# Causal input stage: q, k and v as three rounded products, parts from PSUM, gate logits first, v copied by ScalarE

## The reference, cut to what matters

```python
x = x + s * g                      # s: chunk attention, g: gate of layer 2
xn = _layernorm(x, axis=-1)
# attention of layer 3, input side
qkv = jnp.einsum('btd,ed->bte', xn, w_qkv)
q, k, v = ...                      # 16 heads of 16 channels
# expert choice of layer 3, input side
scores = jnp.einsum('ntd,ed->nte', xn, gate_w)      # 8 experts
probs = jax.nn.softmax(scores, axis=-1)
```

## Time and profile before

| | |
|---|---|
| median of three runs | 3751.04 us |
| profiled execution | 3749.36 us, span 3747.6 us |
| mean granted TensorE clock | 0.908 |
| TensorE, DVE, ScalarE, GpSimd busy | 85%, 81%, 61%, 49% of the span |
| the stage | first instruction at 1662.1 us, the next stage's at 1886.2 |
| first q_parts store of the first and the last batch | 1729.80, 1865.92 |
| DMA packets of the kernel | 478.20 MB, mean 128 GB/s |

### The profile page before, as it was taken

One profiled execution on the slowest core, in us unless ns is written; L12 is line 12 of the kernel. 1 busy time (PEld: TensorE's weight loads), 2 busy tenths in 40 slices (PEclk: granted clock), 3 DMA queues, 4 the chain that ended last, 5 costly groups with the idle time before them and its releaser, 6 DMA issues. The chain is left out here.

```text
span 3747.6 us, 55393 instructions
## 1 busy us (share of the span) xinstructions
PE 3170.5 (85%) x16305; PEld 1686.1 (45%) x16305; DVE 3029.9 (81%) x4822; ACT 2298.3 (61%) x2738; POOL 1834.0 (49%) x915
## 2 busy tenths in 40 slices
PE   6848998888997997878879999899997877777776
PEld 4522333333336886655523434389995631211111
DVE  6969999999995776865669897577768868888887
ACT  5867666667773334743446666522225659999998
POOL 0249998989993111011200000034434448999996
PEclk9879999999998998987879999999998978788888
DMA  3652233333312345955742333134435733344442
GB/s 124 243 203 107 102 146 148 147 124 120 146 49 77 113 150 159 215 140 187 253 139 73 79 73 87 45 95 89 89 62 181 227 115 104 119 124 121 123 119 85
DMA packets 313745, 478.20 MB, mean 128 GB/s; under 512 B 50839, under 2 KB 256280, under 8 KB 293134
## 3 DMA queue, kind: packets, MB, share of 16 engines
q1 hardware_dynamic: 256894, 408.82, 34.2%
q10 hardware_dynamic: 44432, 51.10, 5.1%
q0 software_dynamic: 12288, 16.79, 2.7%
HBM read 322.48 MB, written 153.91 MB: 127 GB/s over the span
## 5 line engine op out<-in xcount | busy, mean ns | idle before, releaser
L1235 PE MATMUL mamba_psum<-mamba_hc,scan_ident 128*128 128x512 f32 x1024 | 552.1, 648 | 86.4 <-DVE mamba_hc L1143 68.6
L3656 POOL TENSOR_TENSOR distance_dist<-distance_dist,distance_least_all 128x2048 f32<-128x2048 f32 x124 | 559.0, 4540 | 77.1 <-DMA distance_least_all<-distance_least_rows 77.1
L1166 DVE TENSOR_TENSOR_SCAN mamba_psum<-mamba_psum,mamba_drive 128x512 f32<-128x512 f32 x352 | 415.4, 1218 | 24.5 <-issue 10.3
L2793 DVE TENSOR_REDUCE causal_row_max<-causal_psum 128x1 f32<-128x512 f32 x512 | 333.3, 683 | 84.7 <-PE causal_psum L2863 71.0
L1235 PEld LDWEIGHTS mamba_psum<-mamba_hc,scan_ident 128*128 128x128 f32 x1024 | 178.1, 197 | 415.4 <-DVE mamba_hc L1143 248.9
L2752 ACT ACTIVATE causal_probs<-causal_psum 128x1024 f32<-128x1024 f32 x256 | 250.7, 1021 | 125.5 <-PE causal_psum L2886 123.6
L3832 PE MATMUL distance_psum<-distance_shared_k_stacks,distance_shared_q_stacks 102*128 102x512 bf16 x512 | 210.8, 508 | 115.0 <-DVE distance_least L3750 55.3
L3750 DVE TENSOR_REDUCE distance_least<-distance_psum 128x2 f32<-128x1024 f32 x256 | 294.4, 1217 | 8.6 <-PE distance_psum L3832 8.4
L3786 DVE TENSOR_SCALAR distance_dist<-distance_psum 128x1024 f32<-128x1024 f32 x192 | 227.1, 1221 | 82.5 <-PE distance_psum L3847 82.5
L1130 ACT ACTIVATE mamba_psum<-mamba_dt,scan_a_neg 128x512 f32<-128x512 f32 x256 | 167.3, 683 | 139.8 <-DVE mamba_hc L1143 139.3
L1130 ACT ACTIVATE mamba_psum<-late_channels,scan_a_neg 128x512 f32<-128x512 f32 x256 | 167.2, 683 | 139.9 <-DVE mamba_hc L1143 129.3
(11 more groups left out here) (473 smaller groups left out, 8734.6 us busy)
## 6 DMA issues: line engine op xcount, KB each, us to landing
distance_least_all<-distance_least_rows SPq DMA_DIRECT2D x32, 1024.0 KB, 4.7
scan_b_all<-bc SPq DMA_DIRECT2D x16, 1024.0 KB, 4.7
scan_c_all<-bc SPq DMA_DIRECT2D x16, 1024.0 KB, 6.6
mamba_b_all<-bc SPq DMA_DIRECT2D x16, 1024.0 KB, 5.0
mamba_c_all<-bc SPq DMA_DIRECT2D x16, 1024.0 KB, 7.0
choice_w<-L_ffn_w SPq DMA_DIRECT2D x16, 1024.0 KB, 5.6
z<-mamba_in_z SPq DMA_DIRECT2D x8, 1024.0 KB, 4.0
xc<-mamba_in_xc SPq DMA_DIRECT2D x8, 1024.0 KB, 4.9
```

The source lines that it names most:

```text
L1166: dve.tensor_tensor_scan(out, bank, drive[:, n % DRIVES], 0.0, ALU.mult, ALU.add).then_inc(h_ready, 1)
L1235: pe.matmul(ps[:, Y_BANK + m % 2], ident[:, :], hc[:, n % PRODUCTS], start=False, stop=(s == DS - 1)).then_inc(y_summed, 1)
L2793: dve.reduce_max(row_max[:, g % 2, u:u + 1], ps[:, u % 2], AX.X).then_inc(a_max, 1)
L3656: pool.tensor_tensor(dist[:, g % 2, kt], dist[:, g % 2, kt], least_all[:, g % 2], ALU.subtract).then_inc(shifted, 1)
```

## The change

- q, k and v: each fp32 product becomes three products of rounded parts, w and xn as `TwoParts`. ScalarE makes a second, rounded copy of each transposed half of xn, DVE the low part.
- `Split` becomes `DirectSplit`: ScalarE casts a tile from PSUM to its high part, DVE subtracts it from PSUM; the fp32 copy in SBUF goes.
- The context is stored in two parts (rounded and rest, 16 rows a batch instead of 8), and one rounded product spreads it.
- The gate logits come first on TensorE in a body, and the rest of the softmax with them; the transposes of probs stand between the two halves of v.
- v is copied by ScalarE. The middle parts stand at the end of ScalarE's body. SyncE stores probs ahead of v.

The core of the diff:

```diff
+        w_parts = TwoParts(c, "w_qkv", [P, DT, 3 * D])
+        xn_parts = TwoParts(c, "xn_t", [P, DT, T])
-        split = Split(c, q_out, k_out)
+        split = DirectSplit(c, q_out, k_out)
...
@@ SyncE
-                    sp.wait_ge(v_copied, b * 2 + 4)
-                    sp.dma_start(token_tiles(v_out, b), ...).then_inc(v_stored, DMA)
                     sp.wait_ge(probs_copied, b + 2)
                     sp.dma_start(probs_out..., probs_t[:, :]).then_inc(probs_stored, DMA)
+                    sp.wait_ge(v_copied, b * 2 + 4)
+                    sp.dma_start(token_tiles(v_out, b), ...).then_inc(v_stored, DMA)
-                means.store_context(sp)
-                load_context(0)
+                sp.wait_ge(y_parts, 2)
+                for j, y_part in enumerate((means.x, means.y)):
+                    sp.dma_start(context_in[:, j * NC:(j + 1) * NC, :], y_part[:, :]).then_inc(means.stored, DMA)
+                sp.wait_ge(means.stored, 2 * DMA)
+                sp.dma_start(context[:, :], context_in[0]).then_inc(loaded, DMA)
...
@@ ScalarE
+                act.wait_ge(turned.copied, len(turned.pairs))
+                for m in range(DT):
+                    act.copy(w_parts.high[:, m], w_turned[m]).then_inc(w_parts.rounded, 1)
                 def turn_copies(b):
                     for m in range(DT):
                         act.wait_ge(xt_done, b * DT + m + 3)
                         act.copy(xn_t[:, m], ps[:, m]).then_inc(xt_copied, 1)
+                        act.copy(xn_parts.high[:, m], ps[:, m]).then_inc(xn_parts.rounded, 1)
                 def body(b, more):
+                    act.wait_ge(shifted, b + 2)
+                    act.activation(lg[:, :, :], lg[:, :, :], ACT.Exp).then_inc(gate_exp, 1)
+                    for n in range(2):
+                        act.wait_ge(qk_done, b * split.TILES + n + 1)
+                        split.act_high(act, b, n, ps[:, 2 + n])
                     if more:
                         ln.act(act, b + 1)
-                    for n in range(split.TILES):
+                    for n in range(2, split.TILES):
                         act.wait_ge(qk_done, b * split.TILES + n + 1)
-                        split.act(act, b, n, ps[:, 2 + n])
-                    split.act_middle(act, b)
-                    act.wait_ge(shifted, b + 2)
-                    act.activation(lg[:, :, :], lg[:, :, :], ACT.Exp).then_inc(gate_exp, 1)
+                        split.act_high(act, b, n, ps[:, 2 + n])
+                    act.wait_ge(turn_done, b + 1)
+                    act.wait_ge(probs_stored, b * DMA + DMA)
+                    act.copy(probs_t[:, :], ps[0:NE2, 1]).then_inc(probs_copied, 1)
+                    act.wait_ge(v_stored, b * DMA + DMA)
+                    for j in range(2):
+                        act.wait_ge(v_done, b * 2 + j + 1)
+                        act.copy(v[:, 2 * j:2 * j + 2, :, 0:HD], ps[:, 6 + j]...).then_inc(v_copied, 1)
                     if more:
                         turn_copies(b + 1)
+                    split.act_middle(act, b)
...
@@ DVE
                 def body(b, more):
+                    if more:
+                        round_context(b + 1)
+                    dve.wait_ge(gate_done, b + 1)
+                    dve.reduce_max(top[:, :], scores, AX.X).then_inc(gate_step, 1)
+                    dve.tensor_tensor(lg[:, :, :], scores, wide(top), ALU.subtract).then_inc(shifted, 1)
                     if more:
                         sums(b + 1)
+                    dve.wait_ge(gate_exp, b + 1)
+                    ...
+                    for n in range(2):
+                        split.dve(dve, b, n, ps[:, 2 + n])
+                    if more:
+                        normed(b + 1)
+                    for n in range(2, split.TILES):
+                        split.dve(dve, b, n, ps[:, 2 + n])
+                    if more:
+                        take_low(b + 1)
...
@@ TensorE
+                    pe.wait_ge(xn_parts.rounded, b * DT + DT)
+                    for i in range(TT):
+                        for m in range(DT):
+                            last = pe.matmul(ps[:, 0, i * NE2:(i + 1) * NE2], xn_t[:, m, i * P:(i + 1) * P], wg[:, m], ...)
+                    last.then_inc(gate_done, 1)
+                    pe.wait_ge(xn_parts.ready, b * DT + DT)
                     for n in range(split.TILES):
-                        split.bank_free(pe, b, n)
                         for m in range(DT):
-                            last = pe.matmul(ps[:, 2 + n], w_qkv[:, m, n * P:(n + 1) * P], xn_t[:, m], ...)
+                            last = three_passes(pe, ps[:, 2 + n], w_parts.both(...), xn_parts.both(...), m == 0, m == DT - 1)
                         last.then_inc(qk_done, 1)
```

More of the change, by code:

```diff
@@ L1943, with __init__ @@
     SELECTS = 4
-    def __init__(self, c, weights, means_in, out):
+    def __init__(self, c, weights, means_in):
         R = self.ROWS
-        self.weights, self.means_in, self.out = weights, means_in, out
+        self.weights, self.means_in = weights, means_in
         self.ident = c.sb("ident", [P, P])
@@ L2374, in stage_causal_in @@
         chunks = c.sb("chunks", [P, TT, D])
-        context = c.sb("context", [NC, D])
+        context = c.sb("context", [2 * NC, D])
+        context_r = c.sb("context_rounded", [2 * NC, D], F32R)
+        y_high = c.sb("y_high", [means.ROWS, D], F32R)
         gate = c.sb("gate", [P, TT, D])
@@ L2438, in body @@
                     if first_groups:
-                        sp.wait_ge(split.stored, (b + 1) * split.STORES * DMA)
+                        split.wait_stored(sp, b)
                         sp.wait_ge(v_stored, (b + 1) * DMA)
@@ L2458, in _ @@
                     sp.wait_ge(stored, (NB + 1) * DMA)
-                sp.wait_ge(split.stored, (NB + 1) * split.STORES * DMA)
+                split.wait_stored(sp, NB)
                 attention.rows_copied(sp)
@@ L2520, in fill @@
                     dve.wait_ge(filled, steps[0])
-                fill(chunk_of[:, :, :], 1.0)
+                for tile in ones:
+                    fill(tile, 1.0)
                 fill(v[:, :, :, :], 0.0)
@@ L2588, in _ @@
                 means.pe_attend(pe, ps)
-                pe.wait_ge(made, 2)
+                pe.wait_ge(made, MADE)
                 pe.sem_inc(xt_done, 2)
                 def spread_context(b):
-                    pe.wait_ge(loaded, (b + 1) * LOADS * DMA)
+                    pe.wait_ge(context_ready, b + 1)
                     for j in range(2):
                         for i in (2 * j, 2 * j + 1):
-                            last = pe.matmul(ps[:, 6 + j, i % 2 * D:(i % 2 + 1) * D], chunk_of[:, i], context[:, :], start=True,
+                            last = pe.matmul(ps[:, 6 + j, i % 2 * D:(i % 2 + 1) * D], chunk_of[:, i], context_r[:, :], start=True,
                                              stop=True)
@@ L3919, in build @@
     given2 = scratch("given2", (NB, T, D))
-    means, context = (scratch(n, (NB, NC, D)) for n in ("means", "context"))
+    means = scratch("means", (NB, NC, D))
+    context = scratch("context", (NB, 2 * NC, D))
     probs2 = scratch("probs2", (NB * NE2, T))
```

118 lines of the change are left out of this document (64 added, 54 removed).

## The result

The changed kernel takes 3769.99 us (median of 6 executions, 3765.38 to 3774.66), the kernel before 3753.10 (6, 3750.41 to 3756.28). The ratio is 1.0045, interval 1.0034 to 1.0055: slower by 13 to 21 us, about 17. The forecast was 3763.7, +12.7. The stage itself, from the first issue for the means to the first issue of the next stage, went from 224.1 to 244.4 us in the two profiled executions. The spans of these two executions differ by as much, 20.4.

What follows compares the result with a forecast made beforehand. TensorE held the loop before; v's store landing would hold it after. 3.8 + 7.1 - 0.6 + 2.4 = +12.7 us, on 3749.4 gives 3762.1, standing for a median of 3763.7; own range 3759 to 3769, 8 in 10 3753 to 3774.

Steps and rivals of the forecast that it cites:

- T: Loop: distance from one batch's first q_parts store to the next; forecast 20.6 us against 19.18 before.
- chain 1: Loop: v's store lands at 15.54, then v copies, xn copies, a middle and low part: 20.6 us a batch.
- chain 2: Loop: high 0 waits for all twelve part stores; landing taken as 2.0 us, xn copies end by 18.7.
- S: Start of a batch's first q_parts store on SyncE; S(b) is that of batch b.
- rival (c): Loop: part stores' landing of 4 us or more leads; T 22.6, +22.7, 3774; with 6, 3784; chance 0.08.
- Loop: S(0) to S(5), five batches: 5 x 20.6 against 95.88 us, +7.1.
- Start: Before the loop: first q_parts store at 1733.6 against 1729.80, +3.8 us; middle parts stand behind next batch's xn.
- S(5) to S(6): After the loop: SyncE waits for v's landing, then issues attention's first loads; 22.6 against 23.2 us, -0.6.
- S(6) to S(7): Stage's end: parts land at S + 13.8, then highs, probs, v, middle and low; 19.5 against 17.05, +2.4.
- Tail: Stage after S(7): claimed to stay as it was.
- The context's chain: Next batch's context lands near S + 20, logits 4 us later, q, k, v by S + 14; off the path.
- Rival (d): Loop: TensorE turns cold; at the lower clock throughout, v at S + 20, T 24.6, 3784; chance 0.04.

Runs made afterwards that it cites:

- The run with other rows: Changed kernel with turned q and k weight columns reordered, so each part's store is 16 rows of 8 pieces, not 8 of 16: ratio 1.0013.

## Why the prediction was right, and where it was not

The sign and the size came out: 3769.99 lies within the bounds for 8 in 10 (3753 to 3774) and 1 us above the forecast's own range (3759 to 3769). The chain that was to make it so did not lead, and the one that did is 0.9 us a batch longer. That the total is this near is in part luck.

- **Sign and kind of mechanism: right.** Every engine has less or little more to do, and T grows, because the middle parts now stand behind a store's landing. The run of ScalarE's order alone shows this on the kernel before; in the changed kernel the waits and the run with a wait per tile show the landing, but bringing the middle parts forward there did not pay, for the reason above.
- **Which landing: wrong.** The forecast let v's landing lead (chain 1, 20.6) and tied chain 2 with it by "I take 2.0" for the parts' landing. Measured: issue by S + 9.2, landing 3.1 to 3.8, then 9.1 us, where the forecast had 9.5 + 2.0 + 9.1. So the term that was mis-sized in this chain is the 2.0, inside its bounds of 2.0 to 6.0. I chose the nearest row by size, a 64 KB store, but it had another shape; with a shape that spreads, the same store lands in 1.7. v itself landed in 4.6 to 6.4 and was there at S + 15.1 (by the median of 5.1), 1.9 ahead of its copy. By mechanism rival (c) is what happened, at a landing shorter than it asked for. The Trainium skill's "Perfetto Trace Analysis", section "DMA Instruction — HWDGE (DVE, Sync)", pointed the right way, that the issue row ends before the data has moved and its semaphore comes late: this trace agrees, with 3.1 to 3.8.
- **Loop:** +7.1 forecast, +13.4 measured (5 x 21.85 against 95.88). Of these 6.3 us 4.4 are the landing (five times 21.47 against 20.6), 1.9 the one landing at S + 13.0 and the two batches in which the context's chain was later.
- **Start:** +3.8 forecast, +4.8 measured (72.5 against 67.7 from the stage's first issue).
- **S(5) to S(6):** -0.6 forecast, +2.0 measured. SyncE did not wait for v but for the next xn, at 1865.83, which stands behind high 0 and so behind the same landing; then attention's fourteen first loads took 8.3 us to issue instead of 7.0.
- **S(6) to S(7):** +2.4 forecast, +0.9 measured. The parts landed at 1887.16, S + 12.5 instead of S + 13.8. **Tail:** 0 forecast, -0.7 measured.
- **Sum:** +12.7 forecast; 4.8 + 13.4 + 2.0 + 0.9 - 0.7 = +20.4 in the profiled pair, about +17 by the medians (13 to 21 by the interval).
- **"What would show it":** stores 20 to 21 us apart: 21.5 to 22.5. v's copy waiting for the DMA of v: no. High 0 waiting for k_parts: yes, in all five. TensorE idle 4 us or more: yes, 5.1 (21.85 less 16.8 busy). First store 4 us later: yes.
- **The context's chain: a second step that failed.** It was left off the path with a cover "1 to 3 us thick". Without the landing's wait T was still 21.22, above the forecast's 20.6, so at 20.6 there was no cover: with the landing forecast as 2.0 and all else as it is, this chain would have held T near 21.2. (The run with other rows has T 20.59, the forecast's number, but by the context's chain with an earlier load.) The terms: the context was to be there near S + 20 and DVE got it at S + 22.0 to 22.8; logits 4 us later, measured 5.2 (1783.65 to 1788.86); q, k and v by S + 14, measured S + 15.8.
- **Rival (d):** the clock did fall. It was 0.73 over the loop against 0.86: 0.50 for the first 9 us of a batch, then 1.00, and 0.50 again from S + 20, when TensorE had gone idle. A third fewer products left T unchanged, so a cold TensorE was not the bound. The Trainium skill's "TensorE: Matmul & The Clock Gate", section "HAM oscillation — how this bites in real kernels", has waits between groups of products return the array to the lower clock again and again: this trace agrees on the clock, and not on the time.

## What to carry to other kernels

When an engine that bounds a loop gets less work, close each buffer's ring by hand, from store issued to store landed to buffer rewritten to store issued again, and price them all: here three lay within 2 us of each other (21.5 to 22.1, 21.2 and 20.0), and single repairs of order and waits gave half a us, which the whole time did not show, while three together, with the context rounded early, gave 3. Take a store's landing from a row of the same shape and the same place in the queue, not the same size. Keep what feeds the next store early in its engine's order, and a small load that an engine waits for ahead of large ones.

## What was not expected of the hardware

- A store's shape bears on how long it takes to land: the last of twelve stores of 128 KB lands 3.1 to 3.8 us behind its issue at a DMA share of 0.5 when written as 8 outer rows, and 1.7 us behind it at 0.6 to 0.7 when written as 16. The issue also got shorter, from 0.77 to 0.69 us on average (9.25 and 8.32 over twelve).
- Gains in such a loop do not add: v's place gave 0.5 us a batch by itself and 1.1 behind the others.
- Rounded products did not make TensorE's share of a batch cheap: 16.8 us busy against 18.4, with the clock at the lower level for the first 9 us of each.
